# Differential attention on one Trainium2 core: the key blocks of a query tile in another order

## What is computed

```python
s1 = jnp.einsum('bhqd,bhkd->bhqk', q1, k1) * scale      # head dim 16
s2 = jnp.einsum('bhqd,bhkd->bhqk', q2, k2) * scale
a1 = jax.nn.softmax(jnp.where(causal, s1, neg_inf), axis=-1)
a2 = jax.nn.softmax(jnp.where(causal, s2, neg_inf), axis=-1)
comb = a1 - lam[None, :, None, None] * a2
out = jnp.einsum('bhqk,bhkv->bhqv', comb, v)            # value dim 32
```

## Time and profile before

| | us |
|---|---|
| median of 3 runs | 2097.22 |
| lowest and highest | 2093.45, 2098.77 |
| the profiled execution | 2093.8 |
| its span on the core | 2091.4 |
| TensorE clock granted, mean share | 0.961 |

### The profile page before, as it was taken

How to read it: one execution, slowest core, us unless ns; L and a number is a source line. 1 busy time by engine, 2 the same in 40 slices (tenths; PEclk the granted TensorE clock), 3 DMA queues, 4 the chain that set the end, 5 groups by cost and what they waited for, 6 DMA issues and landing times. The chain is left out here.

```text
span 2091.4 us, 36204 instructions
## 1 busy us (share of the span) xinstructions
PE 1925.5 (92%) x12400; PEld 1090.7 (52%) x12400; DVE 724.6 (35%) x1543; ACT 1468.2 (70%) x1876; POOL 201.2 (10%) x300
## 2 busy tenths in 40 slices
PE   7994599999899899998999999399999999999997
PEld 5883233333233233332333333278888888888886
DVE  5775021222122221221122212344554535445442
ACT  5663499989899899898998999254444435445452
POOL 0001111111111111111111111000000000000000
PEclk9997699999999999999999999699999999999998
DMA  8997805643366235642564340200101000110000
GB/s 264 361 354 200 134 6 78 83 62 55 51 82 83 36 51 81 83 56 32 79 82 57 52 57 11 81 1 31 31 11 31 22 22 21 33 31 11 11 11 12
DMA packets 137064, 148.83 MB, mean 71 GB/s; under 512 B 76000, under 2 KB 108256, under 8 KB 133760
## 3 DMA queue, kind: packets, MB, share of 16 engines
q1 hardware_dynamic: 134768, 140.55, 33.8%
q10 hardware_dynamic: 1888, 5.24, 1.3%
q0 software_dynamic: 240, 0.66, 0.2%
HBM read 90.85 MB, written 55.57 MB: 70 GB/s over the span
## 5 line engine op out<-in xcount | busy, mean ns | idle before, releaser
L811 ACT ACTIVATE attn_probs<-attn_s_ps 128x1024 f32<-128x1024 f32 (+2 forms) x1152 | 1013.5, 1049 | 112.8 <-PE attn_s_ps L830 106.6
L850 PE MATMUL attn_sums_ps<-attn_probs,heads_v 128*32 128x512 f32 (+3 forms) x5120 | 611.9, 551 | 0.0
L830 PE MATMUL attn_s_ps<-heads_q,heads_k 50*128 50x512 f32 (+3 forms) x2560 | 475.0, 435 | 93.4 <-DMA heads_q<-shift 48.5
L830 PEld LDWEIGHTS attn_s_ps<-heads_q,heads_k 50*128 50x128 f32 x2560 | 218.1, 188 | 577.3 <-ACT attn_probs L811 465.8
L1334 ACT ACTIVATE split_whole<-split_hid_ps,hs 128x512 f32<-128x512 f32 x128 | 88.3, 690 | 274.5 <-PE split_hid_ps L1248 274.3
L895 DVE COPY attn_sums_sb<-attn_sums_ps 128x512 f32<-128x512 f32 x64 | 44.3, 692 | 670.4 <-PE attn_sums_ps L850 666.8
L795 POOL TENSOR_SCALAR_AFFINE_SELECT attn_probs<-attn_probs 128x512 f32<-128x512 f32 x256 | 161.2, 639 | 955.8 <-ACT attn_probs L811 954.6
L1248 PE MATMUL split_hid_ps<-split_hid_b,h2t_r 128*128 128x512 f32 x1024 | 240.6, 392 | 0.0
L1248 PE MATMUL split_hid_ps<-split_hid_a,h1t_r 128*128 128x512 f32 x1024 | 238.1, 391 | 0.0
L1248 PEld LDWEIGHTS split_hid_ps<-split_hid_a,h1t_r 128*128 128x128 f32 x1024 | 190.0, 188 | 41.2 <-DVE split_hid_a L1476 1.4
L1248 PEld LDWEIGHTS split_hid_ps<-split_hid_b,h2t_r 128*128 128x128 f32 x1024 | 189.8, 188 | 38.0
(11 more groups left out here) (123 smaller groups left out, 1567.2 us busy)
## 6 DMA issues: line engine op xcount, KB each, us to landing
qk_parts<-proj_parts SPq DMA_DIRECT2D x64, 512.0 KB, 5.6
heads_q<-qk_parts SPq DMA_DIRECT2D x90, 256.0 KB
heads_k<-qk_parts SPq DMA_DIRECT2D x90, 256.0 KB
proj_w_rows<-in_L_ffn_h_w SPq DMA_DIRECT2D x16, 512.0 KB, 6.5
values<-proj_v SPq DMA_DIRECT2D x8, 1024.0 KB, 6.0
diffs<-attn_diff SPq DMA_DIRECT2D x32, 256.0 KB, 4.5
split_heads<-diffs SPq DMA_DIRECT2D x8, 1024.0 KB, 5.5
heads_v<-values SPq DMA_DIRECT2D x15, 512.0 KB
```

Source lines behind the costliest of these rows:

```text
L811: nc.scalar.activation(weights, side_by_side, ACT.Exp, scale=SCALE).then_inc(exp_done, 1)
L830: last = nc.tensor.matmul(s_ps[n % SLOTS][:, s, place * width:(place + 1) * width], k_sb[u][rows, b * SEQ + j * PARTS:b * SEQ + (j + 1) * ...
L850: last = nc.tensor.matmul(sums[c * D:(c + 1) * D, off:TILE], v_sb[u][:, b * KEY_BLOCKS + j, :], probs[k % PROBS][:, b, s, off:TILE], start ...
```

## The change

In tiles 1 to 3, block 0 comes first, as before; then come the four diagonal blocks in rising order, one behind another, and then the unmasked blocks 1 to 4t - 1. Tile 1 becomes 0, 4, 5, 6, 7, 1, 2, 3; tile 2 0, 8, 9, 10, 11, 1 to 7; tile 3 0, 12, 13, 14, 15, 1 to 11. Tile 0 keeps 0, 2, 3, 1. The lists derived from STEPS (END, UNITS, LAST_UNIT, MASKS) follow.

```diff
     STEPS = [(0, j) for j in (0, 2, 3, 1)]
     for t in range(1, QUERY_TILES):
-        third = SUBS * t // 3
-        order = list(range(SUBS * t)) + [SUBS * t, SUBS * t + 3]
-        order.insert(2 * third + SUBS * t % 3 // 2, SUBS * t + 1)
-        order.insert(third, SUBS * t + 2)
-        STEPS += [(t, j) for j in order]
+        STEPS += [(t, j) for j in (0, *range(SUBS * t, SUBS * t + SUBS), *range(1, SUBS * t))]
     END = [max(k for k, (t, _) in enumerate(STEPS) if t == tile) for tile in range(QUERY_TILES)]
```

## The result

| | before | changed |
|---|---|---|
| median, us | 2095.34 | 2146.63 |
| lowest and highest, us | 2092.71, 2098.77 | 2142.46, 2149.31 |
| span of the profiled execution, us | 2091.4 | 2146.6 |
| TensorE clock granted, mean share | 0.961 | 0.960 |

The changed kernel is slower by 51 us: ratio 1.0242, 95% interval 1.0216 to 1.0268. The forecast was +66 us, to 2163: direction and place were right, the size was some 15 us too large. In the new kernel the lines are four lower: 807 is the exponentials, 826 the scores, 846 the sums, 854 the turn.

A forecast was written before the change was run, and what follows sets the result against it. ACT was taken as the bound, PE closely behind; 16 heads x 4.1 us of added waits gave +66, back edges and first head together 0, on 2093.8: 2160, median 2163 us. Own range 2154 to 2176, widened to 2143 to 2180.

The forecast's parts named there:

- The bound: In the attention, ACT is the bound with PE closely behind; ACT loses only 1.8 us per head to waiting.
- The prices and the chain: Tiles 1 to 3: PE's back-to-back matmul times, summed in program order, make ACT wait 1.44 to 1.65 us before block 1.
- 16 heads x 4.1 = 66 us: Whole attention: waits per head rise from 1.4 to 5.6 us, 4.1 more, over 16 heads +66 us.
- The back edge: Six back edges of the loop over head pairs: PE's 5.53 us standstill, with gain and loss from the new order about cancelling.
- 6 x 0.7 = -4 us: At six back edges, full last units give ACT 1.3 us of cover during PE's standstill, saving 4 us.
- +3 us: After six back edges, a sum grown from 0.35 to 1.00 us falls in PE's slow start: 6 x 0.5.
- The first head: After its 48 us load wait, the first tiles may run at the lower clock: 1 us more, between 0 and 2.
- Covers: POOL's masks, the copy and SP's loads stay hidden at no cost; masks uncovered would cost up to 29 us.
- (a): Rival: nothing changes, ACT's buffers hide the run of diagonal steps, time stays at 2097 us; chance 5%.
- (b): Rival: faster, old waits at tile ends and beside the turn vanish and the run is covered, 2081 us; chance 3%.
- (c): Rival: PE fits the turn in elsewhere, so it hides; 28 us less than forecast, 2135 us; chance 8%.
- (d): Rival: PE's front end feeds the run of diagonal steps too slowly; 29 us more than forecast, 2192 us; chance 7%.

The follow-up runs named there:

- e2_after_plus254: The changed kernel's new order with 254 more idle semaphore instructions on PE ahead of the first head, against the old kernel: 2206.34 us, ratio 1.0532.
- e1_before_plus2: The old kernel's order with two more idle semaphore instructions on PE ahead of the first head, against the old kernel: 2069.43 us, ratio 0.9895.

## Why the prediction was right, and where its size was off

- **The bound.** Right. ACT paces the attention, its work does not change, and all of the difference is its waiting for scores: +53 us of +55.
- **The prices and the chain.** Right. Every distance in tile 1's chain but one is within 0.02 us of the one used; the exception, 0.38 for 0.29 behind the second scores of the 384-wide step, accounts for the 0.07 by which each wait came out short. The waits before block 1 were worked out at 1.44, 1.65 and 1.65 us; measured are 1.51, 1.72 and 1.72 (0.20 of it at the step before, as the chain has it). At (0, 1): 0.72 for 0.60; at (1, 0): 0.19 for 0.27. Sum 5.89 for 5.6 us, and the old order's 1.80 stands where the same working gave 1.43, so comparing like with like was the better of the two readings: 4.09 us a head, predicted 4.1.
- **16 heads x 4.1 = 66 us.** Right: 67.0 us between the two kernels without a loop, 65.4 of it in the profiles' plain heads and 2.7 where the clock fell.
- **The back edge: the mis-sized term.** "6 x 0.7 = -4 us" and "+3 us" were to cancel. The cover was as forecast (ACT had 1.2 us more work than PE at an edge, for 1.3 expected and 0.33 before). But the working took PE's standstill of 5.5 us as fixed. It fell to 2.2 to 2.7 us, because two waits more in the head before the loop moved the loop's first instructions in the 16 KB blocks. That is the step that was wrong in size: -15.5 us where about -1 stood.
- **What the same term left out.** The placement hid a second miss, which shows at equal placement. Over a plain head's time the six heads behind edges take 45.8 us more in the old kernel and 54.9 in e2_after_plus254, both with the long standstills; with the short ones it is 16.5 in e1_before_plus2 and 30.2 in the changed kernel. So the new order costs 9 to 14 us more at its edges, where -1 was worked out: 3 us of it longer standstills, the rest with more time at the lower clock. The placement gives back 25 to 29, and the two together are the -15.5.
- **The accounts of the two profiles.** 16 x 4.09 = +65.4 us; the six heads behind edges take 9.0 us more in all where 24.5 (6 x 4.09) were due, -15.5; the first head +0.9; three heads in which the clock fell in tile 2 or 3, +2.9; an earlier start of the attention, -1.1; the rest of the layer, +2.5. Sum 55.1, spans 55.2.
- **The first head.** Taken at 1 us above its share, it was 0.9.
- **Covers.** Right. POOL released no wait of ACT or PE there, the copy was in time, SP's loads were too.
- **Rivals.** (a), the rule of occupancy, would have left the time as it is, and (b) would have made it faster; the chain of 4.5 us without a gap excludes both. (c) falls with the run in which the turn was moved: it was paid in full. (d), PE's supply inside the run, did not occur: the distances are those of dense stretches. Instructions did matter, but between heads.
- **"The prediction is wrong if the granted clock falls at other places than the six back edges."** It did, at four places in tiles 2 and 3, and at only five of the six edges. The three in heads without an edge cost 2.9 us; with the run in tile 1 alone, such falls cost 6.8 us in five heads. The prediction had no term for it.
- **The ranges.** The time of 2146.6 lies under the forecast's own range of 2154 to 2176. It lies in the wide one, 2143 to 2180, only because that was widened toward rival (c), which did not occur. That the time fell into it is luck; the 4.1 us a head are not.

With both orders at the same place in the instruction stream and the loop kept, the change costs 77 us (2146.6 against 2069.4): 67 for the order, the rest at edges where the clock was at its lower level for 38 us in the changed kernel and for 10 in e1_before_plus2 (one profile of each; why it falls more often in the new order is not shown). The two kernels of this case differ by 51 us because the old one paid 26 us for an unlucky placement that the new one avoided by accident.

## What to carry to other kernels

Where two engines run a pipeline at nearly the same pace, narrow steps are not cheaper in proportion on both: spread them, and keep work that lags behind (here the sums three steps later and the turn five steps later) from falling on them. Such a stall can be worked out to a tenth of a microsecond from the distances between starts in one dense stretch, and it repeats in every tile. A loop's back edge must be read by itself, since its standstill depends on where the loop's first instructions lie, and an edit in front of it moves them; a comparison of two orders is clean only at equal placement or without the loop.

## What the runs showed of the hardware that was not expected

- A loop whose first instruction is the last of a 16 KB block of instructions waits for two blocks at each back edge: 4.7 to 5.5 us for 1.8 to 2.3, in the same order. (That it is the last is inferred, from the 3.03 us between the loop's first two instructions and from the runs with 2 and 256 instructions more.) Two idle instructions ahead of it were worth 26 us in 2095; 254 in the other kernel brought the long standstill back.
- Some 18 us of it were the standstills themselves (29.9 us over the six edges for 11.4), most of the rest the clock: with the short standstills of e1_before_plus2 it stayed at its upper level at three of the six edges, with the long ones at none.
- The granted clock fell to the lower level behind a lull without any standstill (PE busy for 2.65 of 3.41 us, waiting for ACT at each step, no gap above 0.42 us), and in the next head stayed up behind the same lull.
- 254 instructions that only raise a semaphore took PE 39 us, 0.15 us each, and delayed the attention by 34.
